# A transformer chain on one core: the order of work on each engine written out piece by piece

## The reference

```python
x = _L0(x, cond, ctx, ...)  # nx = layer_norm(x); one-head softmax attention over ctx gives evidence
                            # combined = [nx, evidence, anchor]; router softmax over 3 experts
                            # h = silu(combined @ e_w1 + b); routed = sum_e probs_e * (h_e @ e_w2 + b)
                            # x + sigmoid(silu(combined @ gate_w1) @ gate_w2) * (routed @ out_w + out_b)
x = _L1(x, cond, ctx, mask, ...)
x = _L2(x, cond, ctx, ...)
x = _L3(x, cond[:, None, :], ctx, ...)
# each of L1, L2, L3:
#   x += gate * proj(attn16(q, k, v of norm(x)))      self-attention, 16 heads of width 8
#   x += proj(attn16(q of norm(x), k, v of ctx))      cross-attention; L1 masks keys, L2 normalizes ctx
#   x += gate * (gelu(norm(x) @ fc1 + b1) @ fc2 + b2) hidden width 512
# L3 turns q and k by rotary cosines and sines and has no gates
```

## Time and profile before

| | |
|---|---|
| median of 3 runs | 2605.25 us |
| the profiled execution (its span, first to last instruction) | 2610.0 us |
| PE busy | 2315.9 us (89%) |
| DVE busy | 2090.9 us (80%) |
| ACT busy | 1902.6 us (73%) |
| POOL busy | 70.3 us (3%) |
| instructions | 79119 |

### The profile page before, as it was taken

The page is one execution under the profiler, slowest core; times in us unless marked ns, Lnnn a source line. Parts: engine busy times, 40 slices in busy tenths (PEclk is TensorE's granted clock), DMA queues, the critical chain, the costliest instruction groups (busy, mean ns, idle before and its releaser), DMA issues.

```text
span 2610.0 us, 79119 instructions
## 1 busy us (share of the span) xinstructions
PE 2315.9 (89%) x32156; PEld 1828.0 (70%) x32156; DVE 2090.9 (80%) x4845; ACT 1902.6 (73%) x4566; POOL 70.3 (3%) x100
## 2 busy tenths in 40 slices
PE   3989899889988899888999889898899898988897
PEld 3766677667776677766777667776677766766675
DVE  4696887788887888888887878878887788877885
ACT  2577677787777877778777777777786777767875
POOL 0000000000000000000000000000000000000000
PEclk9999999999999999999999999999999999999998
DMA  6000000000100000100010000000000000000000
GB/s 137 32 18 18 13 27 24 28 16 12 32 23 25 16 16 26 30 20 18 14 32 28 18 15 21 26 28 18 16 26 26 27 15 14 23 20 24 14 12 14
DMA packets 99458, 62.90 MB, mean 24 GB/s; under 512 B 32992, under 2 KB 94368, under 8 KB 99104
## 3 DMA queue, kind: packets, MB, share of 16 engines
q1 hardware_dynamic: 90592, 57.80, 7.5%
q10 hardware_dynamic: 8512, 0.03, 0.2%
HBM read 28.31 MB, written 4.29 MB: 12 GB/s over the span
## 4 chain that ended last, share of the span: by engine, by line
PE 51%; DVE 28%; ACT 10%; DMA 4%; issue 4%; SPq 1%; DVEq 0%; ACTq 0%
PE pair L621 11%; PE pair L658 8%; DVE mx L835 7%; DVE wide L837 6%; PE pair L598 6%; PE pair L643 6%; PE pair L674 5%; PE pair L679 4%; DVE wide L831 3%; DMA wide<-probs_by_expert 2%; PE pair L742 2%; ACT wide L781 2%; PE pair L693 2%; DVE stats L715 2%; ACT xn L751 2%
## 5 line engine op out<-in xcount | busy, mean ns | idle before, releaser
L781 ACT ACTIVATE wide<-pair 128x1024 f32<-128x1024 f32 x384 | 391.1, 1023 | 135.0 <-PE pair L658 131.4
L658 PE MATMUL pair<-konst,wide 128*128 128x128 f32 x3072 | 403.7, 275 | 63.7 <-DVE wide L837 42.3
L835 DVE TENSOR_REDUCE mx<-pair 128x16 f32<-128x1024 f32 x320 | 389.6, 1217 | 75.1 <-PE pair L643 73.0
L658 PEld LDWEIGHTS pair<-konst,wide 128*128 128x128 f32 x3072 | 341.1, 141 | 132.3 <-DVE wide L837 77.4
L837 DVE TENSOR_TENSOR wide<-pair,mx 128x1024 f32<-128x1024 f32 x320 | 391.9, 1225 | 10.9
L751 ACT ACTIVATE xn<-pair,table 128x64 f32<-128x64 f32 x896 | 287.3, 408 | 55.3 <-PE pair L742 54.1
L643 PE MATMUL pair<-km,qT 32*64 32x256 f32 x6144 | 222.1, 395 | 89.3 <-DMA km<-kT 20.1
L733 DVE TENSOR_SCALAR wide<-x,mv,rstd 128x128 f32<-128x128 f32 x640 | 190.7, 342 | 52.2 <-ACT rstd L726 48.5
L674 PE MATMUL pair<-wide,vb 128*32 128x64 f32 x12288 | 212.1, 221 | 19.2 <-ACT wide L781 15.0
L674 PEld LDWEIGHTS pair<-wide,vb 128*32 128x32 f32 x12288 | 183.1, 110 | 62.9 <-ACT wide L781 19.4
L643 PEld LDWEIGHTS pair<-km,qT 32*64 32x64 f32 x6144 | 124.9, 133 | 145.7 <-ACT wide L781 22.2
(11 more groups left out here) (219 smaller groups left out, 4329.2 us busy)
## 6 DMA issues: line engine op xcount, KB each, us to landing
km<-kT SPq DMA_DIRECT2D x768, 32.0 KB, 1.8
wide<-probs_by_expert SPq DMA_DIRECT2D x32, 256.0 KB, 2.8
x<-in_x_dram SPq DMA_DIRECT2D x32, 128.0 KB, 2.5
ctx<-in_ctx_dram SPq DMA_DIRECT2D x32, 128.0 KB, 2.2
wide<-probs_by_expert SPq DMA_DIRECT2D x32, 128.0 KB, 3.2
out_dram<-x SPq DMA_DIRECT2D x32, 128.0 KB, 1.9
w0e<-in_L_xcond_e_w_dram SPq DMA_DIRECT2D x4, 384.0 KB, 5.5
w1fc<-in_L_xcond_fc_w_dram SPq DMA_DIRECT2D x2, 256.0 KB, 5.5
```

The lines of the kernel that those rows point to most:

```text
L658: ins = pe.transpose(b[:, t:t + 128], G.ss[:, 2 * c + rr, a:a + 128], ident)
L781: act.activation(G.pT[:, :, 4 * c:4 * c + 4, :].rearrange("k p h q -> k p (h q)"), two_banks(name)[:].rearrange("k (p n) -> k p n", p=2), ...
L835: dve.tensor_reduce(top, heads(s), AX_X, ALU.max).then_inc(*tick("dve", ("max", G.n, tag, c)))
```

## The change

`ORDER` and the rule are gone. `PLACES` gives each piece a number of its own, one for each kind and visit (0 to 7831); `Timetable` goes through the pieces in that one order, appends each to its engine's list, and picks banks with the same `pick` and the same planned costs. Pieces, instructions, waits for data, costs and buffers are the same. The lists of the engines differ: against the lists that the rule makes, 1650 of TensorE's 2816 pieces, 1305 of ScalarE's 2304, 1052 of VectorE's 2304, 206 of SyncE's 312 and 25 of GpSimd's 96 have another index in their engine's list; the mean shift is 1.1 on TensorE, 1.0 on ScalarE, 0.8 on VectorE and 1.1 on SyncE, and the largest is 29. Which banks a piece gets, and so which earlier piece it waits for to free them, follows from the new order. The table loads between ScalarE's pieces are 221 in the old list and 222 in the new one.

The diff, with 15 of the 245 kinds (a line has the places of visits 0 to 31):

```diff
-ORDER = {
-    "in": 9, "c in": -10, "pen": -61.5, "rstd0": 13, "ap0": 20.5, "xn0": -4.5,
-    "k0": -24, "kT0": -12, "probs0": 22.5, "turn0": 92.5, "pd0": -86.5, "evid0": 47.5,
-    "ev0": -54.5, "lg0": -9.5, "rsub0": -6.5, "rexp0": 22.5, "tr0": -7, "pr0": 28,
...
+PLACES = {
+    "in": "1 3 0 2 856 969 1096 1244 1845 1953 2082 2226 2823 2930 3061 3206 3797 3910 4041 4183 4780 4890 5015 5161 5768 5869 6008 6146 6739 6848 6977 7122",
+    "h0": "62 98 104 100 916 1020 1159 1311 1897 2001 2171 2288 2883 2980 3147 3267 3859 3960 4132 4252 4835 4947 5096 5238 5817 5923 6068 6210 6797 6898 7049 7197",
+    "lg0": "60 84 120 82 915 1019 1161 1310 1895 2002 2147 2287 2874 2981 3128 3269 3861 3961 4109 4245 4834 4944 5085 5231 5815 5920 6069 6209 6796 6899 7044 7179",
+    "pre0": "77 108 131 107 931 1032 1164 1312 1899 2006 2172 2303 2887 2984 3158 3278 3860 3971 4137 4256 4841 4958 5107 5245 5825 5925 6083 6217 6802 6907 7055 7200",
+    "rsub0": "70 97 130 126 919 1022 1170 1315 1898 2007 2153 2290 2875 2985 3133 3272 3863 3963 4120 4246 4838 4948 5087 5234 5820 5924 6072 6213 6801 6904 7046 7180",
+    "tr0": "83 118 166 138 924 1027 1180 1324 1906 2013 2164 2294 2882 2993 3146 3280 3867 3967 4128 4253 4845 4952 5098 5241 5826 5931 6078 6219 6811 6912 7062 7192",
+    "spread0": "94 143 189 186 946 1054 1194 1335 1914 2019 2179 2299 2900 3002 3173 3284 3870 3978 4135 4264 4854 4959 5115 5250 5828 5942 6097 6225 6813 6922 7076 7196",
+    "k1s": "169 224 264 268 980 1093 1259 1376 1963 2072 2242 2356 2941 3058 3223 3337 3917 4032 4201 4318 4898 5013 5185 5297 5881 5991 6156 6278 6859 6969 7134 7254",
+    "kT1s": "178 225 265 270 983 1099 1263 1383 1969 2076 2249 2361 2945 3059 3229 3340 3921 4034 4207 4321 4906 5019 5189 5303 5885 5998 6165 6279 6867 6972 7145 7265",
+    "km1s": "185 234 275 276 995 1105 1279 1395 1971 2089 2255 2369 2947 3067 3241 3353 3932 4049 4217 4329 4911 5020 5197 5317 5891 6005 6174 6290 6870 6982 7153 7266",
+    "s1s": "188 251 279 306 1002 1112 1284 1399 1981 2093 2264 2378 2965 3073 3242 3361 3946 4051 4227 4341 4926 5031 5204 5321 5904 6015 6185 6302 6885 6992 7157 7277",
+    "km1x": "233 274 315 316 1053 1192 1306 1425 2092 2178 2297 2461 3001 3172 3283 3375 3977 4133 4263 4356 5021 5113 5230 5343 5945 6095 6226 6315 6983 7077 7195 7288",
+    "s1x": "292 355 377 415 1127 1214 1415 1495 2107 2195 2395 2476 3087 3179 3379 3453 4069 4151 4359 4434 5048 5130 5333 5414 6027 6109 6319 6394 7006 7091 7293 7369",
+    "s2s": "439 513 590 637 1323 1428 1578 1645 2322 2407 2558 2623 3300 3390 3538 3605 4273 4371 4515 4581 5251 5349 5496 5566 6236 6330 6473 6545 7214 7303 7448 7518",
+    "x3": "855 965 1094 1239 1839 1947 2078 2224 2817 2925 3052 3203 3796 3907 4036 4180 4776 4886 5010 5158 5760 5863 5995 6143 6734 6844 6974 7118 7712 7821 7808 7828",
...
@@ -180,40 +388,21 @@
     def __init__(self, pieces):
         self.order = {e: [] for e in ("pe", "act", "dve", "pool", "sp")}
         self.where, self.before, self.begin = {}, {}, {}
-        ends, starts = {}, {}
+        ends = {}
         free = {e: 0.0 for e in self.order}
         bank_free, holder = [0.0] * BANKS, [None] * BANKS
         table = EXP_TABLE
-        ready, waiting, next_of, left = [], {}, {}, {}
-        for p in pieces:
-            waiting[p.name] = len(p.after)
+        places = {kind: [int(p) for p in text.split()] for kind, text in PLACES.items()}
+        for p in sorted(pieces, key=lambda p: places[p.name[1]][p.name[0] - GI]):
+            start = free[p.engine]
             for a in p.after:
-                next_of.setdefault(a, []).append(p)
-            if not p.after:
-                ready.append(p)
-        for p in reversed(pieces):
-            left[p.name] = p.cost + p.lag + HOP + max([left[q.name] for q in next_of.get(p.name, ()) if q.name[0] == p.name[0]], default=0.0)
-        rank = {p.name: p.name[0] * LEAD - left[p.name] + ORDER.get(p.name[1], 0.0) for p in pieces}
-        while ready:
-            best = None
-            for p in ready:
-                start = free[p.engine]
-                for a in p.after:
-                    start = max(start, ends[a][1] + self.hop(ends[a][0], p.engine))
-                banks = self.pick(p.takes, bank_free, start)
-                if banks is None:
-                    continue
-                for b in banks:
-                    start = max(start, bank_free[b] + (TO_PE_HOP if holder[b] else 0.0))
-                if p.table is not None and p.table != table:
-                    start += ACT_TABLE
-                key = (max(start, free[p.engine]), rank[p.name])
-                if best is None or key < best[0]:
-                    best = key, p, banks
-            assert best, "no bank comes free"
-            (start, _), p, banks = best
-            ready.remove(p)
-            if p.table is not None:
+                start = max(start, ends[a][1] + self.hop(ends[a][0], p.engine))
+            banks = self.pick(p.takes, bank_free, start)
+            assert banks is not None, "no bank comes free"
+            for b in banks:
+                start = max(start, bank_free[b] + (TO_PE_HOP if holder[b] else 0.0))
+            if p.table is not None and p.table != table:
+                start += ACT_TABLE
                 table = p.table
             ends[p.name] = p.engine, start + p.cost + p.lag
             self.begin[p.name] = start
@@ -231,11 +420,7 @@
                 for b in range(BANKS):
                     if holder[b] == name:
                         bank_free[b] = start + p.cost
-            for q in next_of.get(p.name, ()):
-                waiting[q.name] -= 1
-                if not waiting[q.name]:
-                    ready.append(q)
-        assert len(ends) == len(pieces), "pieces wait for each other"
+        assert len(ends) == len(pieces), "pieces are missing"
         self.span = max(free.values())
 
     @staticmethod
```

## The result

The changed kernel takes 2579.62 us (median of 6 runs, 2574.49 to 2584.34) against 2605.02 us before: a ratio of 0.9911, 95% interval 0.9891 to 0.993, so 25 us faster. The forecast was 2574 us, its range 2532 to 2608.

A forecast was written before the change was run, and what follows sets the result against it. The prediction took the kernel as bound by TensorE's work plus idle time. Scores 0, turns, mix, norms and projections −25, clock −5.6, SyncE 0 sum to −31 us: 2605.25 − 31 = 2574 us, range 2532 to 2608.

The forecast's parts named there:

- The bound: TensorE's own work plus its idle time, 232.6 us from 100 to 2500 us, forecast to fall to about 205.
- the six groups: TensorE's turns of probabilities, mix, turned norms, turns back and two projections: 123.6 us idle ahead of them, forecast −25.
- Turns, mix, norms, projections (−25): TensorE's waits there, mostly for VectorE or ScalarE, 123.6 us, fall by VectorE's fifth: −25 us, bounds −7 and −62.
- Scores (0, bounds ±15): TensorE's 84.3 us idle ahead of the scores, placed 1.2 us too early, stays: 0, bounds −15 and +15.
- SyncE (0 to +3): SyncE's shifted copies and spreads: one tight copy at visit 29 costs +1 us; 0 to +3 taken.
- Clock (−5.6): A fifth fewer of TensorE's short clock drops, which cost about 28 us: −5.6 us, bounds −28 and +28.
- The tally: Static count per engine of time the order can't cover: TensorE 135.8 to 128.7 us, VectorE 261.0 to 209.7, ScalarE 326.0 to 301.4.
- A: Rival: unready pieces at the head of TensorE's queue hold the list behind them; slower, 2651 us; chance 0.12.
- B: Rival: VectorE and ScalarE gain cover but nothing arrives, as TensorE's own chain ends last; 2602 us; chance 0.11.
- C: Rival: half of the 123.6 us and of the clock drops goes, 2529 us; with a clock-alone neighbour, 2552, chance 0.12.

The follow-up runs named there:

- e7: All five lists searched anew from the changed kernel's places, pieces priced by mean trace durations, key copy at 3.7 us: 2539.04 us, 0.9748 of before.
- e9: Same search and start as e7, but with the key copy priced at the planner's 2.5 us: 2587.53 us, 0.9933 of before.
- e2: Changed kernel with SyncE's list as it was before, the other four lists new: 2595.81 us, 0.9976 of before.
- e5: Changed kernel with only SyncE's list changed, its pieces put where their inputs come: 2568.37 us, 0.9854 of before.
- e4: Kernel before with 300 random swaps of neighbours on one engine that no dependence forbids: 2789.69 us, 1.0717 of before.
- e8: Kernel before, rule and `ORDER` kept, with the key copy's planned lag raised from 2.2 to 3.4: 2866.29 us, 1.0984 of before.
- e10: Search of e7 again from the changed kernel's places, twice its time, four-trace durations, some table loads priced after the wait: 2516.92 us; again 2513.73.
- e1: Kernel before with SyncE's list alone the new one, the other four lists old: 2632.67 us, 1.0122 of before.

## Why the prediction was right, point by point

*The bound.* Right. TensorE's work is the same, and its idle time between 100 and 2500 us went to 207.7, where about 205 was forecast. That these two are so near is partly luck: the six groups fell by 12.6 us more than forecast, and the scores (+8.0) and the small groups (+4.7) made up for it.

*Turns, mix, norms, projections (−25).* Right in its sign and short in size: 123.6 to 86.0, so −37.6. What I under-rated is most likely banks, which I had as the reason of the bound and not in the forecast. By my tally the waits that end with a bank freed by ScalarE fell by 28 us, more than those for VectorE's data (−17), though ScalarE's tally of cover had improved least. The rows' own releasers give less to ScalarE (−20.1) and more to VectorE (−23.0), so the share of each isn't settled. The turns stand 51.8 us, where 50 was forecast. At visit 13 the foreseen wait is gone (VectorE, the gate's sum at L1191 now ahead of the route piece, with no idle time); over the stretch the sums of that line stand 50.0 us idle, 72.4 before:

```profile
1005.70 1.23 DVE L1022 TENSOR_TENSOR wide<-pair,mx 128x1024 f32<-128x1024 f32 x1
1006.84 0.41 DVE L1191 TENSOR_TENSOR wide<-pair,table 128x256 f32<-128x256 f32 x1
1007.36 0.17 DVE L1130 TENSOR_TENSOR small<-pair,route_tok 128x6 f32<-128x6 f32 x1
```

*Scores (0, bounds ±15).* 92.3 for 84.3, +8, inside the bounds. The reason given, a copy counted 1.2 us too short, is what e7 against e9 bears out. At visit 13 the wait is still there, 1.09 us for 1.20. The row names ScalarE's `rstd`, which was over at 1032.93; the copy was issued at 1029.85, and 3.7 us later the scores start:

```profile
1033.54 1.12 PE L828 MATMUL pair<-km,qT 32*64 32x256 f32 x32 [1.09 <-ACT rstd L911]
```

*SyncE (0 to +3).* This term failed. I looked only at copies behind another visit's spread. That one place came out as worked out (+1 forecast, 0.99 measured), but SyncE's list as a whole is worth 17 us to the change (e2 against the changed kernel), and 15 us more were to be had in it (e5).

*Clock (−5.6).* The mean granted clock rose from 0.986 to 0.990, a little more than the 0.988 forecast. TensorE's busy time didn't move with it, but busy time tells little here: e7 has a clock of 0.997 and is busier (2321.4 us) than the kernel before at 0.986. The times of single runs say more. On one chip the unchanged kernel took 2613.43 us in the run with a clock of 0.984 and 2593.12 to 2596.74 in the four with 0.993, a spread nearly as large as the whole gain. At a like clock, 0.992 or 0.993, six runs of the kernel before have a median of 2593.5 us and four of the changed kernel 2576.2. An estimate from these: some 17 of the 25 us are there at a like clock, and some 8 go with the clock. So the term is borne out in its order of size, though idle time and clock go together and no run holds one of them still. (The working has a small slip: half of 58 us is 29, not 28.) Where the order is bad, the clock's part is plain: e4 and e8 have 0.974 and 0.962, and 52.9 and 95.4 us more busy time.

*The tally.* It got the sign right, and the size by luck: e4 shows that it says little of what a misplaced piece costs, and its fall of 7 us on TensorE stands against 25 to 30 us of idle time.

*The rivals.* A didn't come, B didn't come. C, that more than a fifth was to be had, is what e7 and e10 bear out for other places than these.

## What to carry to other kernels

An order that a planner makes is as good as its prices where waits are: find the wait that ends last at the bottleneck, compare its duration in the trace with the planner's number, and search anew with the true one (e7 against e9). Don't correct a price in a rule whose other constants were there for the old one (e8). Don't carry one engine's list over into other lists (e1, e2); mend it with the other lists in place (e5). A static count of uncovered time says little of the time: it rose by 17 us where 300 swaps of neighbours cost 188. And don't trust the releaser that a row names without the times: here the rows name a landing for 24.8 us, where the semaphores give 75.2.

## What the runs showed of the hardware

The granted clock falls as idle time grows, and a bad order pays for both: the mean is 0.997 in e7 and e10, with 215.5 and 196.8 us of idle time in their spans, and 0.962 in e8, with 454.6. A matmul of the scores takes 387, 389 and 406 ns on the mean there, and TensorE's busy time is 2321.4, 2317.7 and 2411.3 us for the same instructions.

A key copy of four DMAs takes 3.7 us from its first issue to its landing: in the kernel before, on the median, 2.4 us of issuing and 1.2 us after that.

A table load starts 0.02 us after the piece ahead of it, also where the piece that needs it still waits (all loads between pieces in the traces of before, the changed kernel, e7 and e10; 270.17 us in the rows above).
